# Place loop of a gather and LSTM kernel: one register load for ten tiles, one-hots in other slots and on another engine

## The reference

```python
support = layernorm(x) @ W_gnn.T + b_gnn
x = x + segment_sum(support[dst] * edge_weight[:, None], src, 6250)
lstm_out = LSTM(layernorm(x))                  # 6250 steps, hidden size 256, i f g o gates
g = argmax(lstm_out @ W_lin.T + b_lin)         # 0 or 1 for each step
w = g * lstm_out;  inc = cumsum(w)
x = x + 2 * lstm_out + (inc - w) * fw_att + (inc[-1] - inc) * bw_att
```

## Time and profile before

| what | value |
|---|---|
| median of 3 runs | 1662.58 us (1661.34 to 1662.65) |
| the profiled execution, its own time | 1660.6 us |
| its span in the trace | 1658.7 us |
| TensorE busy | 1387.2 us, 84% of the span |
| VectorE busy | 1328.6 us, 80% |
| GpSimd busy | 1027.9 us, 62% |
| ScalarE busy | 630.2 us, 38% |
| gathers in the place stage (L630) | 510, of 961 ns each |

### The profile page before, as it was taken

The page is one execution under the profiler, slowest core; times in us unless marked ns, Lnnn a source line. Parts: engine busy times, 40 slices in busy tenths (PEclk is TensorE's granted clock), DMA queues, the critical chain, the costliest instruction groups (busy, mean ns, idle before and its releaser), DMA issues.

```text
span 1658.7 us, 36173 instructions
## 1 busy us (share of the span) xinstructions
PE 1387.2 (84%) x9451; PEld 1213.6 (73%) x9451; DVE 1328.6 (80%) x4070; ACT 630.2 (38%) x2150; POOL 1027.9 (62%) x1087
## 2 busy tenths in 40 slices
PE   6688766777878768988888899888888989999991
PEld 2557764665667637888888888888888888999991
DVE  8899959999999967777878777778878745677765
ACT  0626640000000002444434444443434467777770
POOL 0226547777777777766666666666666400688884
PEclk9799977899999969999999999999999999999995
DMA  9111113333433334444343434334343433443434
GB/s 228 49 50 40 31 17 94 88 89 104 123 88 91 92 99 131 124 135 123 118 140 117 143 113 137 118 119 136 120 145 111 134 111 118 126 123 117 124 100 156
DMA packets 60866, 183.27 MB, mean 110 GB/s; under 512 B 20473, under 2 KB 22049, under 8 KB 59809
## 3 DMA queue, kind: packets, MB, share of 16 engines
q0 software_dynamic: 41312, 98.34, 21.4%
q1 hardware_dynamic: 19500, 84.30, 16.4%
HBM read 141.25 MB, written 41.17 MB: 110 GB/s over the span
## 4 chain that ended last, share of the span: by engine, by line
PE 51%; DVE 17%; issue 8%; DVEq 5%; POOL 1%; ACT 1%; DMA 1%; POOLq 0%; ACTq 0%
PE bank L1986 13%; PE bank L1973 11%; PE bank L1936 8%; PE bank L1888 5%; PE bank L1980 5%; PE bank L1851 4%; DVE big_b L1448 3%; DVE big_a L1204 3%; DVEq L1264 2%; PE bank L1946 2%; DVE big_c L1546 1%; DVE big_c L1407 1%; DVE big_a L1665 1%; DVE big_c L1420 1%; DVE big_a L1199 1%
## 5 line engine op out<-in xcount | busy, mean ns | idle before, releaser
L630 POOL DMA_INDIRECT big_a<-support_scratch,stg_g x510 | 490.1, 961 | 232.9 <-issue 131.4
L1936 PE MATMUL bank<-big_a,big_c 128*125 128x256 f32 x1020 | 296.2, 391 | 9.2 <-DVE big_b L1448 5.0
L583 POOL DMA_INDIRECT big_a<-support_scratch,stg_g x224 | 213.9, 955 | 75.7 <-issue 57.3
L1986 PE MATMUL bank<-big_c 128*128 128x125 f32 x2048 | 256.9, 281 | 4.6 <-DVE big_c L1420 4.6
L1448 DVE TENSOR_TENSOR big_b<-big_b,bank 125x256 f32 x510 | 213.3, 418 | 55.4 <-PE bank L1936 50.6
L1986 PEld LDWEIGHTS bank<-big_c 128*128 128x128 f32 x2048 | 241.4, 191 | 15.4 <-issue 7.2
L1980 PEld LDWEIGHTS bank<-big_c 128*128 128x128 f32 x1600 | 208.9, 192 | 10.8 <-ACT bank L807 0.2
L1973 PEld LDWEIGHTS bank<-xt,w_ih 128*128 128x128 f32 x1600 | 205.2, 192 | 12.0 <-ACT xt L693 4.3
L1536 DVE TENSOR_SCALAR big_c<-consts_sb,listed 128x125 f32<-128x125 f32 x510 | 180.3, 354 | 40.7 <-issue 35.4
L1973 PE MATMUL bank<-xt,w_ih 128*128 128x125 f32 x1600 | 210.0, 275 | 3.4 <-ACT xt L693 3.4
L1980 PE MATMUL bank<-big_c 128*128 128x125 f32 x1600 | 209.4, 275 | 0.0
(11 more groups left out here) (304 smaller groups left out, 2297.9 us busy)
## 6 DMA issues: line engine op xcount, KB each, us to landing
big_c<-gate_input_scratch SPq DMA_DIRECT2D x64, 508.0 KB, 3.5
gate_input_scratch<-pr SPq DMA_DIRECT2D x25, 1016.0 KB, 4.4
big_a<-support_scratch,stg_g POOLq DMA_INDIRECT x734, 2.8
support_scratch<-pr SPq DMA_DIRECT2D x12, 448.0 KB
big_b<-in_x SPq DMA_DIRECT2D x2, 1904.0 KB
out<-big_a SPq DMA_DIRECT2D x2, 1456.0 KB
big_b<-in_x SPq DMA_DIRECT2D x1, 1792.0 KB
out<-big_a SPq DMA_DIRECT2D x1, 1344.0 KB
```

The source lines that it names most:

```text
L583: pool.indirect_dma_start(out=ring[:, s, :], out_offset=None, in_=sup_d, in_offset=bass.IndirectOffsetOnAxis(ap=stg_g[:, q, j:j + 1], axis ...
L630: pool.indirect_dma_start(out=ring[:, s, :], out_offset=None, in_=sup_d, in_offset=bass.IndirectOffsetOnAxis(ap=stg_g[:, r, n:n + 1], axis ...
L1936: mm(bank[4 + POSITION[n] % PSR][0:SEGS, 0:D], oneh[:, s % HELD, 0:SEGS], ring[:, s, :], start=True, stop=True).then_inc(prod, 1)
L1986: return mm(home, w_hh[:, k, g:g + P], h_s[:, q, k, :], start=False, stop=True, skip_group_check=True)
```

## The change

The ten addresses of a place are loaded at its start in one register load (`blocks_of_group`), which reads twelve words. For that the address table is laid out with twelve words for each place from word 224 on, so that it has 836 words in place of 752, is cleared at the start, and is filled by three operations in place of two. The segment one-hots of the next place (`next_sum(0)`, `next_sum(1)`, L1543) move to the slots after the add of tile 2 and after the one-hot that follows the add of tile 3. The one-hots over the 80 support rows (L1546) leave VectorE: ScalarE makes them in `rows_onehot`, as the absolute difference to a row of numbers and then relu(1 - difference), between its copy of the weight sums and its taking of the projection. `sum_weights` waits for two semaphores in place of one.

```diff
+LOADED = 12
+TAB = FULL + 28 * PACE
-        table = sb("table", [1, TILES], i32)
+        table = sb("table", [1, FULL + RUN // PACE * LOADED], i32)
+        by_place = table[:, FULL:].rearrange("o (g n) -> o g n", n=LOADED)
...
+            def rows_onehot(g, r):
+                if not isinstance(g, int) or g >= 2:
+                    act.wait_ge(sum_p, g - 1)
+                for i in range(HOTP):
+                    ins = nc.scalar.activation(hot_dst_1[:, r, i, :], iota[:, 0:HOTROWS], ACT.Abs,
+                                               bias=hot_dst[:, ds(g * HOTP + i, 1)], scale=-1.0)
+                ins.then_inc(dst_a, 1)
+                act.wait_ge(dst_a, g + 1)
+                nc.scalar.activation(hot_dst_1[:, r, :, :], hot_dst_1[:, r, :, :], ACT.Relu, bias=ones[:, 0:1], scale=-1.0
+                                     ).then_inc(dst_r, 1)
...
                     act.wait_ge(sum_p, g + 1)
                     nc.scalar.copy(hot_sum[:, 0:SEGS], bank[5][0:HOTROWS, 0:SEGS]).then_inc(sum_r, 1)
+                if not isinstance(g, int) or g + 1 < NB:
+                    rows_onehot(g + 1, (q + 1 - FIRST) % 2)
                 if h > LAG:
                     take_and_seed(u, q, w)
...
+            V.memset(table[:], 0)
...
-            V.tensor_scalar(table[0:1, 0:512], bank[2][0:1, 0:512], float(SEGL - LEAD), float(D), ALU.add, ALU.mult)
-            V.tensor_scalar(table[0:1, 512:TILES], bank[3][0:1, 0:TILES - 512], float(SEGL - LEAD), float(D),
-                            ALU.add, ALU.mult)
+            V.tensor_scalar(table[0:1, 0:FULL], bank[2][0:1, 0:FULL], float(SEGL - LEAD), float(D), ALU.add, ALU.mult)
+            groups = (TAB - FULL) // PACE
+            V.tensor_scalar(by_place[:, 0:groups, 0:PACE], bank[2][0:1, FULL:TAB].rearrange("o (g n) -> o g n", n=PACE),
+                            float(SEGL - LEAD), float(D), ALU.add, ALU.mult)
+            V.tensor_scalar(by_place[:, groups:, 0:PACE],
+                            bank[3][0:1, 0:FULL + RUN - TAB].rearrange("o (g n) -> o g n", n=PACE),
+                            float(SEGL - LEAD), float(D), ALU.add, ALU.mult)
...
-            regs = [dve.alloc_register(f"tile_block{s}") for s in range(HALF)]
+            regs = [dve.alloc_register(f"tile_block{s}") for s in range(LOADED)]
...
+            def blocks_of_group(g):
+                dve.reg_load(regs, table[0:1, ds(g * LOADED + FULL, LOADED)])
+                return [dve.snap(r, min_val=0, max_val=(NB - 1) * D) for r in regs[0:PACE]]
...
-                vals = blocks_from(0)
+                vals = blocks_of_group(g) if count > 0 else None
                 hot(0)
                 add(0, vals)
...
                 add(2, vals)
+                next_sum(0)
                 hot(3)
...
                 hot(4)
+                next_sum(1)
                 if scaling:
                     squares_of(j, p)
                 add(4, vals)
-                vals = blocks_from(PACE // 2)
...
                     better_guess(j, p, 0)
-                next_sum(0, 0)
                 if scaling:
                     residual(j, p, 1)
...
                 hot(9)
-                next_sum(0, 1)
                 if stepping:
                     state(u, q, 0)
                 add(9, vals)
-                next_sum(1, 0)
                 if stepping:
                     hidden(u, q, 0)
-                next_sum(1, 1)
                 if stepping:
                     products(u, q, 1)
...
-                V.tensor_copy(hot_seg, hot_l)
-                link(V.tensor_copy(hot_dst, hot_i))
+                V.tensor_copy(hot_seg, hot_l)
+                V.tensor_copy(hot_dst, hot_i).then_inc(hot_t, 1)
+                dve.wait_ge(hot_t, 1)
...
                 pe.wait_ge(hot_r, g + 1)
+                pe.wait_ge(dst_r, g + 1)
```

More of the change, by code:

```diff
@@ L358, in build @@
         hot_u = sem("hot_records_out_of_psum")
-        hot_r = sem("hot_onehots_ready")
+        hot_r = sem("hot_segment_onehots_ready")
+        hot_t = sem("hot_records_unpacked")
+        dst_a = sem("hot_row_distances_ready")
+        dst_r = sem("hot_row_onehots_ready")
         sum_p = sem("hot_weight_sums_in_psum")
@@ L888, in _ @@
             act.wait_ge(bits, 1)
+            act.wait_ge(hot_t, 1)
+            rows_onehot(0, 0)
             for h in range(FIRST, 2 * LAG):
@@ L1446, in add @@
                         dve.wait_ge(added, before_us + n + (1 if n >= 7 and summing else 0))
-                        at = acc[0:SEGS, ds(vals[n % (PACE // 2)], D)]
+                        at = acc[0:SEGS, ds(vals[n], D)]
                         V.tensor_tensor(at, at, bank[4 + POSITION[n] % PSR][0:SEGS, 0:D], ALU.add).then_inc(added, 1)
@@ L1455, in add_sum, with next_sum @@
                         V.tensor_tensor(at, at, bank[4][0:SEGS, 0:D], ALU.add).then_inc(added, 1)
-                def next_sum(i, of):
+                def next_sum(i):
                     if not isinstance(g, int) or g + 1 < NB:
-                        hot_onehot(g + 1, 1 - r, i, of)
-                def blocks_from(n):
-                    return blocks(first + (TFROM[1] + n), PACE // 2) if n < count else None
-                vals = blocks_from(0)
+                        hot_onehot(g + 1, 1 - r, i)
+                vals = blocks_of_group(g) if count > 0 else None
                 hot(0)
@@ L1537, in place_onehot, with hot_onehot @@
                                 ALU.is_equal, ALU.mult).then_inc(oh_r, 1)
[L1539 to L1549, removed]
+            def hot_onehot(g, r, i):
+                if i == 0 and (not isinstance(g, int) or g >= 2):
+                    dve.wait_ge(sum_p, g - 1)
+                ins = V.tensor_scalar(hot_seg_1[:, r, i, 0:SEGS], iota[:, 0:SEGS], hot_seg[:, ds(g * HOTP + i, 1)],
+                                      hot_w[:, ds(g * HOTP + i, 1)], ALU.is_equal, ALU.mult)
+                if i == HOTP - 1:
+                    ins.then_inc(hot_r, 1)
             def unpack_hot():
@@ L1569, in _ @@
             for i in range(HOTP):
-                for of in range(2):
-                    hot_onehot(0, 0, i, of)
+                hot_onehot(0, 0, i)
             for h in range(FIRST, 2 * LAG):
@@ L1805, in _ @@
             pe.wait_ge(ge_done, 1)
-            mm(bank[2][0:1, 0:512], turn[:], tile_ge[0:NB, 0:512], start=True, stop=True)
-            mm(bank[3][0:1, 0:TILES - 512], turn[:], tile_ge[0:NB, 512:TILES], start=True, stop=True)
+            mm(bank[2][0:1, 0:TAB], turn[:], tile_ge[0:NB, 0:TAB], start=True, stop=True)
+            mm(bank[3][0:1, 0:TILES - TAB], turn[:], tile_ge[0:NB, TAB:TILES], start=True, stop=True)
             for p in range(2):
```

## The result

The changed kernel takes 1622.49 us (median of 4 runs, 1615.00 to 1625.07), the kernel before 1662.62 us beside it (4 runs, 1661.34 to 1663.96). The ratio is 0.9751, with a 95% interval of 0.9717 to 0.9785: faster by 2.5%. 1617 us was forecast, with a range of 1605 to 1640. The profiled execution took 1623.77 us, with a span of 1621.9 us.

A forecast was written before the change was run, and what follows sets the result against it. TensorE was taken as nearly the bound, idling at the weight sum for VectorE's last one-hot. A place falls from 14.44 to 13.45 us, 45.5 us over 46 places: 1617 us, range 1605 to 1640.

The forecast's parts named there:

- L1546: Support-row one-hots leaving VectorE: 0.34 us less; with the other moves TensorE's 1.12 to 1.53 us weight-sum wait is covered entirely.
- what is late next: TensorE's projection waits for ScalarE's copy into `xt`, behind tile 8's add, cell state and tanh: a chain of 13.4 us.
- the projection to tile 8: TensorE's stretch from projection to tile 8, first link of the `xt` chain: 10.59 us, from a place in the old loop.
- The load: One twelve-word register load a place on VectorE: 0.6 us taken from the eight-word load, upper end 2.8 us.
- L1980 waiting for L807: Sign of being wrong: TensorE's LSTM weights at L1980 wait for ScalarE's seed L807.
- The tie of the two chains: ScalarE's seed chain, 13.4 and 12.9 us, ties with the `xt` chain every second place; 0.05 us added, 13.45 us a place.
- in further pieces: Bound for the twelve-word load: 1.2 us if more than eight words are fetched in further pieces; 1631 us, chance 0.12.
- piece by piece: Bound for the twelve-word load: 1.8 us if it is fetched piece by piece at four words.
- The slower rival: Load at 237 ns a word, 2.8 us: 15.35 us a place, 1705 us; decides from about 1.9 us on; chance 0.06.
- The second register load: VectorE's mid-place load goes, and its 1.15 us stall with it, out of the half place in which VectorE is late.
- ScalarE's new work: Abs and relu one-hots on ScalarE ahead of the seed: 1.0 us a place, bounds 0.8 to 1.3 us.
- The sum: 0.99 us saved in each of 46 places, 45.5 us in all; nothing counted for the places before 636 us.

The follow-up runs named there:

- onehots_only: The changed kernel with the two five-word loads and the old address table; 1941.52 us, ratio to the kernel before 0.9783, and 0.9815 when run again.
- load_only: The kernel before with the twelve-word table and one load a place, its one-hots left on VectorE; 1979.67 us, ratio to the kernel before 0.9975.
- ten_words: The changed kernel with table rows of ten words, without the two of padding, and a ten-word load a place; 1986.57 us in one run.

## Why the prediction was right, and where it was off

**L1546, and what is late next: right.** The weight sum waits for nothing (its 1.12 and 1.53 us were covered entirely), and `onehots_only` shows on the other chips that this is the gain. What is late next is `xt`, as said. The chain was put at 13.38 us; it is 13.56 and 13.59 us in the timeline. From projection to tile 8 it was 10.59 us and is 10.68 and 10.84. The other links, forecast and then measured in the first place: tile 8 to its add 0.82 and 0.83; add to cell state 0.99 and 1.05; to the tanh 0.32 and 0.31; to the copy 0.21 and 0.21; to the projection 0.45 and 0.48.

**The term that was mis-sized is the projection to tile 8.** The distance was taken from a place in which the projection followed the weight sum without a wait. After a wait its first group takes 0.99 us to the next tile (1020.17 to 1021.16), in every place of the changed kernel that has the wait. In all 47 places of the old trace without it, it took 0.89 us, and in the first with it, at 1313.85 us, 0.99. That is 0.1 us a place that the stall for `xt` brings with it. In the second place another 0.16 us follow.

**The load.** Those 0.16 us are the seed: TensorE's weights wait 0.29 us for L813, and such a wait of 0.24 us or more stands 18 times between 700 and 1260 us. That is one of the prediction's own signs of being wrong (L1980 waiting for L807), and it holds in these 18 of 41 places. The tie of the two chains was thus seen, and in the place with the loop's turn, as forecast, but the seed's chain is the longer one there: from the add of tile 8 to the first one-hot are 3.71 us (1018.12 to 1021.83), where 3.2 was forecast. Of the 0.5 us, 0.25 are the load, 0.85 us and not 0.6; 0.1 are the taking of the registers (0.55 us from the end of the load to the one-hot, where 0.40 before and 0.05 more were counted); the rest lies ahead of the load. Twelve words are three whole fours, and the third costs 0.25 us. The bounds "in further pieces" and "piece by piece" priced each further piece like a whole load, 0.6 us, though eight words in 0.60 us already held two of them. By the prediction's own rule the 0.25 us make 13.65 us in one place and leave 13.4 in the other, 13.53 us in the mean. From add to add of tile 8 the trace has 13.72 us (1018.12 to 1031.84) and 13.44 us (1004.68 to 1018.12), and the stretch 13.52 us a place.

**The slower rival: its mechanism is real.** A load of 2.29 us exists, at 0.22 us a word, and is passed on; twelve words from a start that is a multiple of four don't pay it. The layout with twelve words a place, and not ten, is what keeps the change from it. It was put to decide from 1.9 us on; `ten_words` is even at a mean of 1.67 us, on another chip and from one run.
The Trainium skill ("Runtime: NRT & Kernel Launch", section "Instruction fetch mechanics") puts about 200 ns on each register, in bulk too; it speaks of loads from HBM, while the table here lies in SBUF. The runs come near that figure for words that count singly (0.22 us) and not for whole fours from an aligned start (0.06 us a word).

**The second register load: wrong as a reading.** "From the load to L1546 VectorE sets the pace" did not hold up to tile 8, where VectorE only ties with TensorE; it sets the pace from the add of tile 8 on. `load_only` took the stall away, and a quarter of a per cent came of it. The sum did not rest on it, since the new period was built from the chain that remained and not by taking stalls away from the old one. Had the saving been summed from the stalls, the one of 1.15 us would have been counted for a gain that it did not bring.

**ScalarE's new work: right.** The abs groups take 0.61 us for two and the relu 0.43; 0.98 us in all (1.0 forecast), and from the first one-hot to the take 2.44 us (1.45 + 1.0).

**The sum.** The stage gave 42.2 us, 45.5 were forecast: 0.07 us x 46 = 3.3 us. Between the profiled executions the miss is 8.8 us (1623.77 against 1615), between the medians 5.5 (1622.49 against 1617). The rest of it is ahead of the stage, where the sum counted nothing: the first load of the loop over the first 224 tiles began 3.2 us later (261.1 against 257.9 us), and the stage 5.3 us later. The runs of the changed kernel spread over 10 us, those before over 3, so part of it may be the single execution's. The laying out of the table is 0.5 us of it, since it ends at 74.4 us and not at 73.9. What the rest is stays open.

## What to carry to other kernels

Build the period that remains from the chain that is late next, link by link, instead of subtracting stalls: a stall on the chain of waits can lie beside the pace, if the engine waits for another one further on. A stall that moves to a new place brings a restart with it (0.1 us here). Give tables that are read into registers a row length and a start of whole fours: with the two words of padding a load takes 0.85 us here, and without them 1.06 and 2.29 us in turn. Where the profile names a tile that an instruction can't have waited for, look for a register load behind it.

## What the runs showed of the hardware beyond this

The price of a register load goes by aligned fours, as worked out above.

A second load of the same registers right behind the first left no second load in the trace.

On the chips of the experiments the other engines wait long for TensorE's results. In the stage of the changed kernel ScalarE idles for more than 3.5 us 67 times there, up to 8.4 us, and never on the chip of the result. One such wait, for the LSTM products (its releaser is not in the trace; TensorE's rows have the products done at 1179.32 us):

```profile
1186.64 0.38 ACT L845 ACTIVATE big_c<-bank 128x250 f32<-128x250 f32 x1 [8.17 <-remote]
```

From 1182 us on TensorE's passes are single, with up to 1.15 us between them for which the profile names nothing. The granted clock is still 1.00 from 1184 to 1185 us and falls within the wait, to 0.50, the 1.2 GHz level, where it stays up to 1192 us:

```profile
1184.00:1185.00 1.00, 0.00 (x0) 0.00 (x0) 0.00 (x0) 0.00 (x0) 0.68 (x1) 1.00 0.46 131
1185.00:1186.00 1.00, 0.48 (x1) 0.21 (x1) 0.00 (x0) 0.00 (x0) 0.00 (x0) 0.61 0.43 131
...
1187.00:1192.00 5.00, 3.88 (x13) 2.80 (x13) 4.53 (x20) 1.52 (x8) 1.92 (x2) 0.50 0.09 26
```

The stage of the changed kernel takes 903.6 us there and 660.8 us on the chip of the result, while all that lies behind it takes the same time (318.8 and 319.5 us). What makes those waits was not found.
